# Cross-attention kernel: the projection's subtraction ahead of the head work on GpSimd, and the unscaled lower weight pieces from VectorE to GpSimd

## The reference

```python
ln_out = _ln(hidden_states, ln_w, ln_b)
q  = _ln(_fp8_linear(ln_out, wq, wq_scale, q_in_scale))      # 16 heads of 128
k  = _ln(_fp8_linear(ln_out, wk, wk_scale, k_in_scale))      # 8 groups of 128
v  = _fp8_linear(ln_out, wv, wv_scale, v_in_scale)
core = _gqa(q, k, v)
qx = _ln(_fp8_linear(ln_out, wqx, wqx_scale, qx_in_scale))
kx, vx = split(einsum('bsi,oi->bso', cond, w_kv_x)); kx = _ln(kx)
xout = _gqa(qx, kx, vx)
catq = _div_clamp_fp8(concatenate([core, xout]), proj_smooth)
x = x + einsum('bsi,oi->bso', catq, wproj) * (proj_in_scale * proj_w_scale)
```

## Time and profile before

| | |
|---|---|
| median of 3 runs | 1187.11 us (1186.66 to 1187.77) |
| the profiled execution's own time | 1185.83 us |
| its span | 1184.0 us |
| busy in the span: PE, PEld | 894.8 us (76%), 785.4 us (66%) |
| busy: DVE, ACT, POOL | 957.7 us (81%), 723.2 us (61%), 401.2 us (34%) |
| attention stage, 266 to 1074.5 us | 808.5 us, of which PE 716.02 us busy |

### The profile page before, as it was taken

The page is one execution under the profiler, slowest core; times in us unless marked ns, Lnnn a source line. Parts: engine busy times, 40 slices in busy tenths (PEclk is TensorE's granted clock), DMA queues, the critical chain, the costliest instruction groups (busy, mean ns, idle before and its releaser), DMA issues. The chain is left out here.

```text
span 1184.0 us, 22559 instructions
## 1 busy us (share of the span) xinstructions
PE 894.8 (76%) x6878; PEld 785.4 (66%) x6878; DVE 957.7 (81%) x2509; ACT 723.2 (61%) x2536; POOL 401.2 (34%) x602
## 2 busy tenths in 40 slices
PE   3620576218878799878879988888899999997638
PEld 3620243217777688767778877777799999996627
DVE  7989898788888899788889877777788888886461
ACT  3442244647777777677777766666777777774313
POOL 0029000003343433344343444444444443433124
PEclk9855598559999999999999999999999999999559
DMA  6030000111001011000101100000000000000400
GB/s 216 1 107 0 0 1 0 36 47 34 2 1 37 2 37 37 2 1 1 37 1 37 46 10 10 10 10 10 10 15 11 15 10 15 11 6 1 147 19 19
DMA packets 24292, 29.97 MB, mean 25 GB/s; under 512 B 1584, under 2 KB 19824, under 8 KB 23920
## 3 DMA queue, kind: packets, MB, share of 16 engines
q1 hardware_dynamic: 23792, 27.51, 7.1%
q0 software_dynamic: 384, 1.05, 0.3%
HBM read 25.93 MB, written 2.62 MB: 24 GB/s over the span
## 5 line engine op out<-in xcount | busy, mean ns | idle before, releaser
L1477 PE MATMUL a_pj_ps<-wp,a_cat 128*128 128x256 f32 x1024 | 157.6, 297 | 91.8 <-POOL a_cat L1231 91.8
L1254 DVE TENSOR_REDUCE a_v<-a_sq 128x6 f32<-128x768 f32 x128 | 121.8, 951 | 116.1 <-ACT a_sq L1407 115.9
L1477 PEld LDWEIGHTS a_pj_ps<-wp,a_cat 128*128 128x128 f32 x1024 | 131.0, 192 | 112.5 <-POOL a_cat L1231 105.9
L1231 POOL TENSOR_TENSOR a_cat<-a_tb,a_mb 128x512 fp32r<-128x512 bf16 x128 | 147.6, 1153 | 63.5 <-DVE a_tb L1293 61.5
L1389 ACT ACTIVATE a_p<-a_kT_sc_ps,a_nmax 128x64 f32<-128x64 f32 x512 | 151.5, 307 | 2.9 <-DVE a_nmax L1261 2.9
L1443 PE MATMUL a_qo_ps<-wq,a_xqf 128*128 128x512 f32 x512 | 151.2, 417 | 0.0
L1218 POOL TENSOR_TENSOR a_pn<-a_p,a_rsum 128x256 f32<-128x256 f32 x128 | 78.8, 616 | 183.8 <-DVE a_rsum L1338 183.8
L1400 ACT ACTIVATE a_sq<-a_kv_ps 128x256 f32<-128x256 f32 x128 | 49.2, 384 | 135.2 <-PE a_kv_ps L1505 66.9
L1535 PE MATMUL a_kT_sc_ps<-a_kT,a_qT 128*128 128x64 f32 x1024 | 128.8, 269 | 0.6 <-ACT a_kT L1403 0.6
L1535 PEld LDWEIGHTS a_kT_sc_ps<-a_kT,a_qT 128*128 128x128 f32 x1024 | 124.3, 192 | 1.2 <-ACT a_qT L1395 1.0
L1389 ACT ACTIVATION_READ_ACCUMULATOR a_p<-a_kT_sc_ps,a_nmax 128x1 f32 x512 | 103.3, 202 | 0.0
(11 more groups left out here) (315 smaller groups left out, 2197.5 us busy)
## 6 DMA issues: line engine op xcount, KB each, us to landing
a_ctx<-in_ctxT SPq DMA_DIRECT2D x32, 128.0 KB, 2.2
w_work<-in_wprojT SPq DMA_DIRECT2D x3, 1024.0 KB, 5.7
x_res<-in_x SPq DMA_DIRECT2D x4, 512.0 KB, 5.4
vT<-in_ctxT SPq DMA_DIRECT2D x2, 1024.0 KB, 9.8
w_work<-in_wqxT SPq DMA_DIRECT2D x2, 1024.0 KB, 5.0
w_work<-in_wkvxT SPq DMA_DIRECT2D x4, 512.0 KB, 4.6
out_x<-x_res SPq DMA_DIRECT2D x4, 512.0 KB, 4.6
tf_work<-in_wqT SPq DMA_DIRECT2D x1, 1024.0 KB, 6.5
```

The source lines that it names most:

```text
L1231: nc.gpsimd.tensor_tensor(cat[out8.n % 2][:], tb[:], mb[:], ALU.subtract).then_inc(cat_ready, 1)
L1254: norm(nc.vector.tensor_reduce(v6[:], sq[:].rearrange("p (h d) -> p h d", d=D), AX.X, ALU.add))
L1477: last = nc.tensor.matmul(pj_ps[:, pj.turn % 2, :], cat[pj.n % 2][:, a * P:(a + 1) * P], wp[part][:, pj.half * HU + a, :], start=(pj.half ...
```

## The change

GpSimd's step gets another order: `pn`, then the lower part of the weight piece if it has no scale (moved here from VectorE), then `cat`, then the head, then `convert`. Before, the head came ahead of `cat`. VectorE keeps only the pieces with a scale. Counts and semaphores stay the same; GpSimd waits for the same `piece_upper` count as VectorE did, and in addition for the lower part of the piece before.

```diff
                             rsum[:].unsqueeze(2).broadcast_to([P, 4, S]), ALU.mult).then_inc(pn_ready, 1)
+                    w, count = piece(u, FIRST_LOWER_AT) if u.live else (None, None)
+                    if w and w.scale is None:
+                        pool.wait_ge(aw["piece_upper"], count)
+                        pool.wait_ge(aw["piece_lower"], count - 1)
+                        nc.gpsimd.tensor_tensor(w.lower, w.raw, w.upper.bitcast(F32), ALU.subtract
+                                                ).then_inc(aw["piece_lower"], 1)
+                    if out8.live:
+                        pool.wait_ge(cadd_ready, out8.count())
+                        wait_unit(pool, pj_done, out8.before(2))
+                        nc.gpsimd.tensor_tensor(cat[out8.n % 2][:], tb[:], mb[:], ALU.subtract).then_inc(cat_ready, 1)
                     head = head_item(u) if u.live else None
                     if head:
                         pool.wait_ge(aw["head_scaled"], head.count)
@@
-                    if out8.live:
-                        pool.wait_ge(cadd_ready, out8.count())
-                        wait_unit(pool, pj_done, out8.before(2))
-                        nc.gpsimd.tensor_tensor(cat[out8.n % 2][:], tb[:], mb[:], ALU.subtract).then_inc(cat_ready, 1)
@@
                         w, count = piece(now, FIRST_LOWER_AT)
-                        if w:
+                        if w and w.scale is not None:
                             dve.wait_ge(aw["piece_upper"], count)
-                            if w.scale is None:
-                                nc.vector.tensor_tensor(w.lower, w.raw, w.upper.bitcast(F32), ALU.subtract
-                                                        ).then_inc(aw["piece_lower"], 1)
-                            else:
-                                nc.vector.scalar_tensor_tensor(w.lower, w.raw, w.scale, w.upper.bitcast(F32), ALU.mult,
-                                                               ALU.subtract).then_inc(aw["piece_lower"], 1)
+                            nc.vector.scalar_tensor_tensor(w.lower, w.raw, w.scale, w.upper.bitcast(F32), ALU.mult,
+                                                           ALU.subtract).then_inc(aw["piece_lower"], 1)
```

## The result

The changed kernel takes 1085.88 us (median of 4, 1084.42 to 1087.46) against 1187.44 us for the kernel before in the same comparison; the ratio is 0.914, 95% interval 0.912 to 0.916. The profiled execution took 1087.46 us with a span of 1085.7, the slowest of the four.

The account below looks back on a forecast made before the run. TensorE was idle in head steps, waiting for `cat` behind GpSimd's wait for ScalarE's head. Savings of 27.6, 30.9, 34.8 and 0.8 us, together 94.1, gave 1091.7, or 1093.0 as median; range 1087.5 to 1105.

Parts of the forecast that it names:

- `cat` ahead of the head: On GpSimd in head steps: `cat` starts once `tb` is ready, so TensorE's wait of 1.23 us goes.
- The lower part: Moved to GpSimd: takes 0.73 us, ends 1.63 us after `rsum`'s start, delays `cat` by at most 0.1 us.
- Contention, `tb`: On VectorE: `tb` waits for GpSimd's lower part, ending 2.04 us after `rsum`'s start; unheld, 3 us less.
- floor case: Head steps all at 5.37 us, 5.86 in phase 2: 4.6 us less, 1088; chance 0.12.
- VectorE's own round: VectorE's step with holds by GpSimd: 5.45 us on average in phases 0 and 1, 5.90 in phase 2.
- The floor: TensorE's least time for a step: 5.37 us in phases 0 and 1, 5.86 in phase 2.
- The sum: Attention stage savings: 27.6, 30.9 and 34.8 us in phases 0 to 2, 0.8 in headless piece steps; together 94.1.
- the one from a profiled execution to a median: Whole kernel: profiled execution forecast at 1091.7 us, raised by 1.3 to a median of 1093.0; 0.5 allowed for scatter.
- `tb` is not held and the holds are hidden: Rival for head steps: every step at 5.37 or 5.86 us, 4.6 us less, 1088; chance 0.12.
- The steps at the lower clock: Two phase 2 steps at clock 0.81 return to full clock, some 1.4 us each, contained in phase 2's saving.

Follow-up runs that it names:

- Order alone: Kernel before with only GpSimd's order changed, `cat` ahead of the head, lower parts left on VectorE: 1088.93 us, ratio 0.918.
- no centring: Kernel before, old order, GpSimd leaving out both head instructions and not waiting for ScalarE's head: 1091.14 us, ratio 0.922.
- the run with zeros: Changed kernel with unscaled lower parts filled with zeros by a GpSimd memset in place of the subtraction: 1087.00 us.
- lower part behind `cat`: Changed kernel with GpSimd's lower part behind `cat` instead of ahead of it, still before the head: 1092.82 us, ratio 0.921.
- more on TensorE: Changed kernel with both key transposes on TensorE done twice in each of the 128 units: 1116.07 us.
- Less on TensorE: Changed kernel with the query product's second pass left out, two of four matmuls in each of the 128 units: 1072.05 us.
- The run with 0.33 us more on VectorE ahead of `rsum`: Changed kernel with VectorE's `mb` computed twice in each of the 128 units, the second time ahead of `rsum`: 1094.66 us, ratio 0.925.

## Why the prediction was wrong, by its own steps

*`cat` ahead of the head*: right. The wait is gone, the head hides. Order alone and no centring show it from both sides.

*The lower part*: 0.74 us measured for 0.73. That it delays nothing is shown by the run with zeros. But its end was added up wrongly: 0.24 + 0.61 + 0.73 is 1.58 us after `rsum`'s start and not 1.63; 1.57 was measured.

*Contention, `tb`*: it was held, 0.65 us beside the lower part against 0.41 to 0.42 in the runs without one beside it (zeros, lower part behind `cat`). "SBUF — State Buffer" of the Trainium skill (section "SBUF: two separate sides") has it so, by its lock of the shared port pair. The trace agrees that `tb` is held. The term was mis-sized: `tb` ends 0.28 us after the lower part, not 0.41, so 1.85 us after `rsum`'s start, not 2.04. And what it is worth was put at 3 us, where the prediction's own floor case makes it 4.6; the run with zeros shows 0.2.

*VectorE's own round*: this is the step of the mechanism's pricing that failed, and the largest term of the miss. I put 5.38, 5.53, 5.37 and 5.53 for four steps and took their mean, 5.45. Measured over four steps are 4.97, 4.98, 5.39 and 5.20. The mis-sized terms are the hold of `tb` (0.24 instead of 0.44) and above all `convert`'s, at 0.37 twice in four steps. It is 0.24 in one of four, with L1287 at 0.53 instead of 0.29 (timeline of the changed kernel):

```profile
350.45 0.83 POOL L1202 CAST a_xqf<-xq 128x768 fp32r<-128x768 bf16 x1
...
350.90 0.53 DVE L1287 TENSOR_SCALAR a_yb<-a_yb 128x512 bf16<-128x512 bf16 x1
```

In the other it is nothing: there `convert` starts at 361.03, after L1261, and runs out at 361.86 while L1287, started at 361.70, still takes 0.30. I had taken a worst hold for a typical one without placing `convert` in the step. With a mean of 5.13 VectorE stays under the floor, and the one step that ends on it has a short one behind it. The run with 0.33 us more on VectorE ahead of `rsum` shows that little more would have made my figure true: its steps are 5.50 on average in phase 1.

*The floor*: 5.37 to 5.40 and 5.87, right; more on TensorE shows that it is one. Less on TensorE shows that it is a floor with others 0.1 us beneath.

*The sum*, by profiles: phase 0 gave 28.5 us (142.07 to 113.57) for 27.6, phase 1 32.6 for 30.9, phase 2 35.5 for 34.8, the piece steps 0.6 for 0.8. That is 97.2 for 94.1, so VectorE's round accounts for 3.1 of the 7.1 us by which the forecast missed; 1.1 came from outside of the stage: 98.3 in the span. The remaining 2.9 are a second step that failed, the one from a profiled execution to a median: before it lay 1.3 us under its median, after 1.6 over it. I allowed 0.5 for that. With VectorE's round alone put right the forecast would have been 1089.9, and with the step to the median alone 1090.1, both inside the range; it took the two together, 1087.0, to leave it.

*The rivals*: "`tb` is not held and the holds are hidden" at 1088 came closest, with the wrong half: `tb` is held and it is hidden. The steps at the lower clock vanished as forecast: none of the eleven profiles in which the head no longer holds up `cat` has one in the stage, the other two have two and three.

Not tried: whether these steps, which come and go between profiles, make the scatter of the kernel before, 1180.1 to 1189.7 over all comparisons. One costs 1.5 us.

## What to carry to other kernels

When an in-order engine waits for late, unurgent work ahead of short, urgent work, changing the order alone can be worth nearly all: here 96.7 us of 99.5, against 2.8 for 68 instructions moved to the idler engine. Before pricing contention, place both instructions in the step: a held instruction costs only what exceeds the spare time of its engine, and that the same 0.74 us cost nothing ahead of `cat` and 5 us behind it is a matter of what they meet. And a forecast for a median made from one profile needs the scatter of both kernels in its range: here the changed kernel's executions lie up to 1.6 us from its median, and those of the one before spread over 9.6.

## What the runs showed that I had not expected

A few elements suffice to be held: L1280 works on 128x6 values and took 0.58 us beside `pn` when an instruction ahead of it made it 0.2 us late, 0.13 otherwise. So from the start of `rsum` to `qn` it took 0.93 us instead of 0.26. The whole round grew by less where `tb`, now later, no longer met the lower part: by 0.43 us, with `tb` back at 0.41.

A PE that is busy 100% of a window isn't by that alone the only bound: with 0.46 us taken off its query product, the steps fell by 0.09 to 0.12 only, while 0.22 us more on it made them 0.21 to 0.22 longer.
